# New step orders on all engines of a two-layer attention and expert kernel

## The reference, cut to what matters

```python
# layer 0, attention: 16 heads of width 128, a state per head
q, k, v = (silu(causal_conv(xn @ W.T, taps)) for W in (Wq, Wk, Wv))
beta = sigmoid(xn @ Wb.T);  q = l2norm(q) * hd**-0.5;  k = l2norm(k)
pred  = k_t @ state
state = state + k_t ^ (beta_t * (v_t - pred))        # for each token
o_t   = q_t @ state
out   = rmsnorm(o) * rms_w @ Wo.T
# layer 0, experts: 2 of 8 by a grouped router, and a shared one
# layer 1, attention: 2 heads, weights w0, w1, w2 learned on the way, chunks of 64
gate, hb = ki @ w0, ki @ w2;  hidden = silu(gate) * hb
w_m = w_m + newtonschulz5(gradient_m)                # 2 steps each, m = 0, 1, 2
w_m = w_m / (norm(w_m) + 1e-5) * norm(w_m at start)
oi  = silu(qi @ w0) * (qi @ w2) @ w1
out = rmsnorm(o) * onorm_w @ W_proj
# layer 1, experts: 2 of 6 for each whole sequence, gelu
```

## Time and profile before

| what | us |
|---|---|
| median of 3 runs | 1775.88 (1772.57 to 1785.23) |
| the profiled execution | 1781.47 |
| its span, first to last instruction | 1779.7 |
| PE busy | 1692.1 (95%) |
| DVE busy | 1470.7 (83%) |
| ACT busy | 1206.8 (68%) |
| POOL busy | 1104.7 (62%) |

### The profile page before, as it was taken

One profiled execution on the slowest core, in us unless ns is written; L12 is line 12 of the kernel. 1 busy time (PEld: TensorE's weight loads), 2 busy tenths in 40 slices (PEclk: granted clock), 3 DMA queues, 4 the chain that ended last, 5 costly groups with the idle time before them and its releaser, 6 DMA issues.

```text
span 1779.7 us, 41654 instructions
## 1 busy us (share of the span) xinstructions
PE 1692.1 (95%) x14070; PEld 1247.5 (70%) x14070; DVE 1470.7 (83%) x3684; ACT 1206.8 (68%) x2911; POOL 1104.7 (62%) x1148
## 2 busy tenths in 40 slices
PE   7999899999999999999999999999988788888888
PEld 5577567777777777777777777777767566666667
DVE  5322599999999999999999999999986788888863
ACT  2134477777777777777777777877754588778763
POOL 1600067777777777776666666666666478778841
PEclk9999999999999999999999999999986699999999
DMA  9433310111110110100001000101002000000033
GB/s 313 148 96 110 105 31 22 38 31 27 36 33 27 30 36 21 39 18 27 27 18 27 24 18 24 30 12 30 15 2 60 1 1 1 2 1 1 1 89 91
DMA packets 66098, 73.85 MB, mean 41 GB/s; under 512 B 10975, under 2 KB 54767, under 8 KB 65775
## 3 DMA queue, kind: packets, MB, share of 16 engines
q1 hardware_dynamic: 62919, 63.92, 12.2%
q0 software_dynamic: 3072, 8.65, 1.5%
HBM read 55.45 MB, written 17.10 MB: 41 GB/s over the span
## 4 chain that ended last, share of the span: by engine, by line
PE 84%; DVE 8%; ACT 5%; issue 1%; POOL 1%; SPq 0%; DMA 0%; POOLq 0%; DVEq 0%; ACTq 0%
PE banks L735 19%; PE banks L893 6%; PE banks L762 4%; PE banks L849 3%; PE banks L770 3%; PE banks L868 3%; PE banks L778 3%; PE banks L700 3%; PE banks L807 3%; PE banks L815 2%; PE banks L821 2%; PE banks L949 2%; PE banks L814 2%; PE banks L1025 2%; PE banks L719 2%; PE banks L960 2%
## 5 line engine op out<-in xcount | busy, mean ns | idle before, releaser
L735 PE MATMUL banks<-xnT,hw 128*128 128x512 f32 x768 | 414.1, 622 | 2.5 <-DVE cv L2034 2.5
L2090 DVE CAST_PREDICATED MM<-lmask,banks 128x512 bf16<-128x512 uint32 x384 | 272.5, 710 | 35.8 <-PE banks L815 31.5
L2034 DVE SCALAR_TENSOR_TENSOR cv<-banks,hc,cv 128x510 f32<-128x510 f32 (+2 forms) x384 | 284.8, 742 | 5.5 <-ACT cv L1439 0.8
L1503 ACT ACTIVATE T<-banks 128x256 bf16<-128x256 f32 x384 | 149.3, 389 | 147.4 <-PE banks L807 147.1
L2694 POOL TENSOR_TENSOR X<-X,yrow 128x512 f32<-128x512 f32 x128 | 163.3, 1276 | 66.3 <-ACT yrow L1535 66.3
L2658 POOL TENSOR_TENSOR kn<-nsum,half_pos 128x4 f32<-128x4 f32 x64 | 65.6, 1025 | 142.2 <-DVE nsum L2059 142.2
L815 PEld LDWEIGHTS banks<-MM,T 128*128 128x128 bf16 x1536 | 104.3, 98 | 65.4 <-issue 48.4
L814 PEld LDWEIGHTS banks<-T,MM 128*128 128x128 bf16 x1280 | 99.1, 97 | 65.3 <-ACT T L1503 63.1
L2034 DVE SCALAR_TENSOR_TENSOR cv<-banks,hcv,cv 128x510 f32<-128x510 f32 (+2 forms) x192 | 141.4, 736 | 1.4 <-ACT cv L1439 1.3
L893 PE MATMUL banks<-ho,OT 128*128 128x256 f32 x512 | 141.7, 400 | 0.0
L807 PEld LDWEIGHTS banks<-MM,Gb 128*128 128x128 bf16 x1536 | 84.2, 98 | 81.3 <-issue 43.7
(11 more groups left out here) (318 smaller groups left out, 4885.9 us busy)
## 6 DMA issues: line engine op xcount, KB each, us to landing
MM<-in_eye SPq DMA_DIRECT2D x64, 256.0 KB, 2.7
slot_rows<-zeros SPq DMA_DIRECT2D x1, 5304.0 KB, 20.1
xs<-slot_rows SPq DMA_DIRECT2D x13, 408.0 KB, 4.0
slot_out<-ye SPq DMA_DIRECT2D x13, 384.0 KB, 2.7
hw<-in_hw SPq DMA_DIRECT2D x16, 256.0 KB, 3.4
wT<-in_winit SPq DMA_DIRECT2D x8, 384.0 KB, 3.9
wgu<-in_wgu SPq DMA_DIRECT2D x1, 2816.0 KB
w1c<-in_ew SPq DMA_DIRECT2D x16, 176.0 KB
```

What stands on the lines that cost most here:

```text
L735: ins = pe.matmul(PROJ[t][:], hw[:, kk, t, :], xnT[:, kk, u.b * BLK:(u.b + 1) * BLK], start=(kk == 0), stop=(kk == KD - 1))
L1503: act.activation(strips(T1[:].rearrange("p i t -> p (i t)"), LEVELS[lv], 0, 1), grams_bank(u)[:, 0:TILES * 64].rearrange("p (k e) -> p k e ...
L2034: dve.scalar_tensor_tensor(o, y, taps_of(t)[:, TAPS - 1 - i:TAPS - i], o, ALU.mult, ALU.add).then_inc(dve_conv, 1)
L2090: dve.copy_predicated(dst, m, ps).then_inc(dve_mm, 1)
```

## The change

No instruction of the computation is added or taken away. The lists of steps are new: on PE, ACT, DVE and POOL in the first attention's period, in the last units and what lies between the stages, in the second attention's `pair_period`, and in the tail. Each list now also begins at another step of the cycle, so that a name such as `u3` can stand for the same unit as `u2` did. POOL's list goes up to two units further back (`mask`, `gram_rest` and the fetched rows come one period later), and its loop ends earlier, with `a59` and `a60` spelled out. `units` takes the number of units as an argument. Four waits are new: SP waits for all inversion steps before it loads the last pair's weights, `project_out` of the last two units waits for `act_ot`, `project_qk` of a first chunk waits for the turned rows itself, and POOL waits for its own addition of fetched rows.

```diff
-        def units(h, j):
-            return [unit(h, j, back) for back in range(5)]
+        def units(h, j, backs):
+            return [unit(h, j, back) for back in range(backs)]
...
             sp.wait_ge(*weights_loaded(2))
+            sp.wait_ge(pe_inv, 13 * UNITS)
             load_weights(3)
...
+                    pe.wait_ge(act_ot, u.n + 1)
                     if s == 1:
                         pe.wait_ge(act_bv, UNITS)
...
-                do(invert, u2, 5)
-                do(gram_keys, u1)
-                do(invert, u2, 6)
-                do(first_solve, u3, 1)
-                do(gram_second, u1)
+                u0, u1, u2, u3 = units(h, j, 4)
                 do(times_gram, u3, 1, 0)
                 do(invert, u2, 7)
                 do(project, unbegun(u0), QRY, 0)
                 do(invert, u2, 8)
+                do(correct, u3, 1, 0)
                 do(project, unbegun(u0), KEY, 0)
-                do(correct, u3, 1, 0)
                 do(invert, u2, 9)
                 do(project, unbegun(u0), QRY, 1)
...
+                do(invert, u1, 4)
                 do(correct, u2, 0, 1)
-                do(invert, u1, 4)
                 do(project_out, u3, 1)
                 do(carry, u2)
-
+                do(invert, u1, 5)
+                do(gram_keys, u0)
+                do(invert, u1, 6)
+                do(first_solve, u2, 1)
+                do(gram_second, u0)
             pe.wait_ge(a_const, 3 * 16)
             pe.wait_ge(*a_eye)
...
                     pe.wait_ge(t_wk2, u.n - NP + 1)
+                else:
+                    pe.wait_ge(ln_kept0, NBLK + u.p + 3)
...
+                do(newton, u3, 0, 0, NEXT)
+                do(newton, u4, 1, 1, GRAM)
+                do(grads, u2, 1)
+                do(newton, u4, 1, 1, SQUARE)
+                do(newton, u3, 0, 1, TURN)
+                do(project_v, u1)
+                do(newton, u4, 1, 1, NEXT)
+                do(newton, u3, 0, 1, GRAM)
+                do(turn_weight, u4, 0)
+                do(turn_output, u5)
+                do(total, u2)
                 do(newton, u3, 0, 1, SQUARE)
                 do(turn_qk, u1)
                 do(turn_weight, u4, 1)
-                do(project_rows, u5)
                 do(newton, u3, 0, 1, NEXT)
                 do(turn_v, u1)
+                do(project_rows, u5)
                 do(gate_queries, u4)
                 do(gates, u1)
                 do(newton, u3, 1, 0, TURN)
+                do(hidden_back, u1)
                 do(newton, u3, 1, 0, GRAM)
-                do(hidden_back, u1)
                 do(newton, u2, 0, 0, TURN)
                 do(newton, u3, 1, 0, SQUARE)
+                do(turn_weight, u4, 2)
                 do(turn_mixed, u4)
-                do(turn_weight, u4, 2)
+                do(newton, u2, 0, 0, GRAM)
                 do(newton, u3, 1, 0, NEXT)
-                do(newton, u2, 0, 0, GRAM)
+                do(project_qk, u0)
+                do(newton, u3, 1, 1, TURN)
+                do(newton, u2, 0, 0, SQUARE)
                 do(output, u4)
-                do(project_qk, u0)
-                do(newton, u2, 0, 0, SQUARE)
-                do(newton, u3, 1, 1, TURN)
                 do(grads, u1, 0)
-                do(newton, u3, 1, 1, GRAM)
-                do(newton, u2, 0, 0, NEXT)
-                do(grads, u1, 1)
-                do(newton, u3, 1, 1, SQUARE)
-                do(newton, u2, 0, 1, TURN)
-                do(project_v, u0)
-                do(turn_output, u4)
-                do(newton, u3, 1, 1, NEXT)
-                do(newton, u2, 0, 1, GRAM)
-                do(turn_weight, u3, 0)
-                do(total, u1)
             pe.wait_ge(t_const, 5 * 16)
...
+                do(keep_first, u3, 1)
                 do(silu, u1, VAL)
+                do(invert, u2, 4)
                 do(square_queries, u1)
                 do(invert, u2, 5)
                 do(cross_keys, u1)
+                do(gram_half, u1)
                 do(tap0, unbegun(u0), QRY)
-                do(gram_half, u1)
                 do(invert, u2, 6)
                 do(tap0, unbegun(u0), KEY)
+                do(first_queries, u1)
...
@@ -1693,95 +1706,94 @@
                 do(half_tanh, u1)
                 do(silu_gate, u1)
                 do(newton, u3, 1, 0, GRAM)
+                do(newton, u2, 0, 0, TURN)
+                do(keep_weight, u4, 2)
                 do(square_weights, u3, 0)
-                do(newton, u2, 0, 0, TURN)
+                do(newton, u2, 0, 0, GRAM)
                 do(keep_mixed, u4)
-                do(keep_weight, u4, 2)
-                do(newton, u2, 0, 0, GRAM)
+                do(newton, u3, 1, 1, TURN)
+                do(silu_qk, u0)
+                do(square_qk, u0)
                 do(square_outputs, u4)
-                do(silu_qk, u0)
-                do(newton, u3, 1, 1, TURN)
-                do(square_qk, u0)
...
                 do(key_inverse, u1)
                 do(invert, u2, 4)
                 do(key_scales, u1)
+                do(gram, u1, 0)
                 do(refine, u3, 1, 0)
-                do(gram, u1, 0)
                 do(gram, u1, 1)
...
-            residual(a62, 1, 1)
-            sum_qk(x0)
             refine(a62, 1, 1)
             rates_end(0)
+            norm_qk(x0, 0)
+            norm_qk(x0, 1)
+            residual(a63, 0, 0)
+            norm_qk(x0, 2)
+            refine(a63, 0, 0)
             norm_rows(1, 1)
-            residual(a63, 0, 0)
...
-                do(rhs_minus, u2, 0, 1)
-                do(inverse_rms, u3)
-                do(add_rows, u3, 0)
-                do(rhs_minus, u2, 1, 0)
-                do(first_rhs, u1)
-                do(root, u0)
-                do(mask, u1)
-                do(rhs_minus, u2, 1, 1)
-                do(add_rows, u3, 1)
-                do(gram_rest, u0)
-                if 0 <= i <= TOP0 * NT:
-                    do(rows_added, u3)
-                merge(i)
-                do(rhs_minus, u1, 0, 0)
-
+                u0, u1, u2, u3, u4, u5, u6 = units(h, j, 7)
+                do(add_squares, u5)
+                do(rhs_minus, u4, 0, 1)
+                do(inverse_rms, u5)
+                fetch_rows(i - 3)
+                do(rhs_minus, u4, 1, 0)
+                do(mask, u4)
+                add_fetched_rows(i - 4, u6, 1)
+                do(root, u2)
+                do(first_rhs, u3)
+                do(rhs_minus, u4, 1, 1)
+                fetched_rows_added(i - 4)
+                do(add_rows, u5, 0)
+                do(gram_rest, u3)
+                do(add_rows, u5, 1)
+                do(rhs_minus, u3, 0, 0)
             pool.wait_ge(a_const, 3 * 16)
             pool.wait_ge(m_added, 2 * NBLK)
...
             def pair_period(n):
                 u0, u1, u2, u3, u4, u5 = pair_units(n)
+                do(update, u4, 2)
+                do(root_grads, u2)
+                do(root_weights, u4, 1)
+                do(scale_weights, u4)
+                do(update, u3, 0)
+                do(update, u3, 1)
+                do(one_minus, u1)
+                do(rate_keys, u1)
+                do(root_weights, u3, 0)
                 do(rate_hidden, u1)
-                do(root_weights, u3, 0)
                 do(inverse_output, u4)
                 do(root_qk, u0)
                 do(scale_weights01, u3)
-                do(update, u3, 2)
-                do(root_grads, u1)
-                do(root_weights, u3, 1)
-                do(update, u2, 0)
-                do(update, u2, 1)
-                do(scale_weights, u3)
-                do(rate_keys, u0)
-                do(one_minus, u0)
             def weight_roots():
...
             rate_keys(x0)
             add_rows(a62, 0)
-            rhs_minus(a63, 1, 0)
-            rhs_minus(a63, 1, 1)
+            mask(a63)
             add_rows(a62, 1)
+            norm_root(2, 1)
             rate_powers(1)
             add_squares(a63)
-            norm_root(2, 1)
```

More of the change, by code:

```diff
@@ L2409, in gate_logits @@
                 dve.tensor_tensor(lg[:], lg[:], lmx[:].unsqueeze(2).to_broadcast([1, NB, E1]), ALU.subtract).then_inc(dve_once, 1)
+            tap(a63, VAL, 1)
+            invert(a62, 1)
+            square_sums(a60)
+            residual(a61, 0, 1)
+            refine(a61, 0, 1)
+            invert(a62, 2)
+            tap(a63, VAL, 2)
             second_rhs_half(a61)
```

582 lines of the change are left out of this document (310 added, 272 removed).

## The result

The changed kernel takes 1801.10 us in the median of 4 runs (1799.54 to 1807.90), the kernel before 1775.42 (1772.57 to 1785.23). The ratio is 1.0149, 95% interval 1.0105 to 1.0193. The forecast was 1767 us with a range to 1790, so it was wrong, and on the wrong side of no change. The profiled execution of the changed kernel took 1801.76 us, its span 1800.0 us, 20.3 us more than the span before.

What follows compares the result with a forecast made beforehand. It took the first attention as bound by PE, the second by a ring of waits, the stretch between by latency and a low clock. +5 - 17 + 3 = -9 us gave 1772.5 profiled, 1767 from the median; range 1747 to 1790.

Steps and rivals of the forecast that it cites:

- POOL in the first attention: First attention: mask, low Gram half and fetched rows come up to one period later; POOL has slack, so priced at nothing.
- Rival (B): Pair steps: DVE steps slowed beside POOL's updates give back 1.1 of 1.4 us each; about 1780 us, chance 0.17.
- PE's list: First attention: two moves put 128-column matmuls ahead of long float32 groups, 0.06 us less per unit, 4 us for 60.
- tap0 behind Gb: First attention, ACT: query tap 0.57 us later delays DVE; 0.15 us per unit reaches PE, 9 us, bounds 0 and 0.5.
- DVE's Gk ahead of the refinement: First attention, DVE: `gram` 0 ahead of a `refine` makes KX earlier but not the last Gk; no separate price.
- Sum for the first attention: PE's gain and the query tap's delay together: +0.09 us for each of 60 units, +5 us, bounds -4 and +26.
- Rival (C): First attention: DVE's 0.5 us delay behind the late query tap reaches PE whole; +26 us, about 1788 total, chance 0.13.
- The late weight load that costs nothing: First attention: a load waited 0.42 us for DVE at 712.59 while PE's long matmuls did not stop.
- Second attention: Pair steps: w1p ahead of squares and th, NEXT ahead of GRAM shorten the ring; 12 x 1.4 = 17 us less.
- The lower bound: Pair steps: gain of 0 if another order-bound ring of the old length takes over.
- Between the stages: Later rate power costs 4.9 us, `residual` ahead of row tiles gains 1.4; +3 us taken, bounds -3 and +7.
- Tail: End of the kernel: new order of nearly independent work, 0, within 2 us either way.

Runs made afterwards that it cites:

- e7: Kernel before with PE's two moves (correction, inversion step 4) and POOL's early key mask, in the first attention: units 17.87 us apart, ratio 1.0158.
- e12: Kernel before with POOL's early mask and only PE's correction moved ahead of the key projection: units 17.87 us apart, ratio 1.0162.
- e1: Changed kernel with POOL's key mask put back late in the first attention: units 17.62 us apart, ratio 1.0046 to the kernel before.
- e6: Kernel before with only PE's two moves (correction, inversion step 4) done in the first attention: units 17.40 us apart, ratio 0.9981.
- e18: e10 with PE's two moves (correction, inversion step 4) done in the first attention: 1750.90 us, ratio 0.9867 to the kernel before.
- e10: Kernel before up to pair step 2, changed kernel's pair steps and tail from pair step 3 on: 1754.45 us, ratio 0.9918.
- e2: Changed kernel with ACT's first query tap ahead of the half Gram matrix again: units 17.91 us apart, ratio 1.0138 to the kernel before.
- e17: Changed kernel with POOL's mask late and DVE's refinement ahead of the key-mask product again: units 17.50 us apart, ratio 0.9997 to the kernel before.
- e13: Changed kernel with POOL's mask, PE's two places and DVE's refinement put back: units 17.49 us apart, ratio 0.9989 to the kernel before.
- e5: Changed kernel with POOL's mask and PE's two places put back: units 17.63 us apart, ratio 1.0045 to the kernel before.
- e15: Kernel before with only DVE's first key-mask product moved ahead of the second chunk's refinement: units 17.59 us apart, ratio 1.0054.
- e11: Kernel before with only ACT's copy T of inversion step 3 moved behind both pieces of scaled rows: units 17.39 us apart, ratio 0.9992.
- e8: Changed kernel with two pieces between the stages put back (POOL's rate power; DVE's rates end and expert choice): ratio 1.0110 to the kernel before.
- e4: Kernel before with only POOL's key mask moved early in the first attention: units 17.50 us apart, ratio 1.0014.

## Why the prediction was wrong, point by point

**POOL in the first attention, "so I take nothing": the step that failed.** The prediction asked who reads the mask's result, and how busy POOL is. It did not ask which DVE step lies beside the mask at its new place. The named risk, that the mask would hold up `outputs`, was another one. The price is the wait at L821: 0.46 us a unit together with the moved correction (e7, e12), 0.29 in the changed kernel (e1). Rival (B) had the kind of effect, DVE beside POOL, but looked for it in the pair steps and at instructions of two SBUF inputs. In the trace a one-input step, 128x4, was stretched most. The trace of before already had such a case: `norm_qk` 0, which also adds a constant to 128x4 numbers, beside POOL's scaling of a weight. "SBUF — State Buffer" of the Trainium skill, section "SBUF: two separate sides", has a GpSimd instruction, and a VectorE instruction in a 2-port mode, take a shared pair of ports as an exclusive lock for the whole instruction; a VectorE instruction with two SBUF inputs does so against a GpSimd one that reads SBUF. By it `nsum` would wait for the mask's end; the trace agrees (1011.36 against 1011.32), but no run here shows in which mode that step runs.

**PE's list, -0.06 us a unit.** Alone it measured -0.01 to -0.02 (e6, and e18 against e10). No run shows the reason given, that the projection's weights can't be loaded behind so short a matmul. The prediction treated the moved correction as a matter of matmul shapes and did not look up how long its input had been ready. That was 0.76 us, a number that could have been read from the trace of before.

**tap0 behind Gb, +0.15 a unit.** Nothing in the changed kernel (e2), where PE waits at L821 anyway. DVE's first query tap waits 0.19 us for it and no more.

**DVE's Gk ahead of the refinement.** The prediction saw the move, took from it that KX is earlier, and gave no price to the refinement that now stands behind 0.6 us of Gk. It costs 0.12 to 0.17 us a unit (e17 against e1, e13 against e5, e15). Sum for the first attention: +5 predicted, with an upper bound of +26; +30 measured. The bound was too low because it was taken from one wait alone.

**Rival (C), 17.9 us apart and about 1788 or more.** Its sign came true, by a different cause; that (C) with (B)'s loss gave 1801, the measured time, is luck. The sign was therefore a bad one: it could not tell the mechanisms apart.

**The late weight load that costs nothing**, 0.42 us in the earlier trace rows, was read rightly: T's late load in e11 is a second case. What the reading missed is that Rb's lateness passes this cover. At L821 the load waits 0.45 us on the mean of 47 in e12's trace, and PE's matmul 0.34.

**Second attention, -17 us.** The size came true: 252.55 - 235.83 = 16.7 us, 1.39 for each of 12 periods where 1.4 was taken, at 19.65 us on the mean (19.7 predicted), PE at 94% (over 92% predicted). The mechanism is right in part, and no run takes its pieces apart. `square_weights` and w1p, which were on the chain of each period, are on it in none of the changed kernel's. But in 8 of the 12 periods, 19.2 us long, the chain there runs through another ring, over the squares of the gradients on ACT and their root on POOL (`root_grads`, gnb). Two rounds of it, start, us, what:

```profile
1504.19 2.45 POOL gnb L2786
...
1523.41 2.45 POOL gnb L2786
```

The lower bound had named such a ring, at the old length. And "DVE's part keeps its work: 0" missed `norm_qk` 0 (nq), 0.34 us shorter in the changed kernel. Before (with POOL's step beside one of them, 1463.03 to 1463.53) and changed:

```profile
L2232 DVE TENSOR_SCALAR nq<-nqr x16: 151/500/575, 1335.1 to 1674.5; 128x4 f32<-128x4 f32 x16
...
1461.47 2.04 POOL L2782 TENSOR_TENSOR wT<-wT,wsc 128x512 f32<-128x512 f32 x2
```

```profile
L2246 DVE TENSOR_SCALAR nq<-nqr x16: 150/161/171, 1370.3 to 1700.5; 128x4 f32<-128x4 f32 x16
```

So the fall of 1.39 on 1.4 is partly luck: the sum of the old ring is not what sets most of the new periods. Rival (B)'s `norm_qk` 2 takes 996 ns in the median, no more than before.

**Between the stages, +3 us, up to +7.** The sign of the loss was right, the size and most of the place were not. The rate power of pair 1 starts at 1392.17 with DVE waiting 5.28 us, as foretold; but counted from `keep_output` of unit 60 it starts at 67.6 us where it started at 54.8, 12.7 us later and not 4.9. Most of that is lost in the last three units. There the prediction took 1.4 us of gain from `residual` standing ahead of the row tiles. The single wait of 3.36 us for Rb did go, but the new order has PE wait 5.4 us for the inversion's merges where it waited 1.4, and the three units take 7.9 us more. In the two profiles the whole stretch is 8.9 us longer. Nine kernels with the old order here took 117.4 to 124.6 us (mean 120.1), ten with the new one 132.7 to 135.0 (133.8): 14 us. The profile of before had the longest of the nine, at the lowest granted clock (0.74, the others 0.78 to 0.81), which hid part of the loss. e8 explains 2.6 of the 14, the last three units hold some 8; which moves in them cost it is not settled.

**Tail, 0 within 2.** It gained 4.3 us against the profile of before. It takes 105.9 to 106.1 us in every kernel that has the new order there, 108.7 to 110.4 with the old one.

**The sum.** With the measured terms, 30 + 14 - 17 - 4 = +23 us, against 26 from the ratio (0.0149 x 1775). The gain in the pair steps was real; it was more than paid for in the first two stages.

## What to carry to other kernels

When a step is moved on one engine, write down for its new place which instructions of the other engines run beside it there (a step moved on POOL lengthened one on DVE from 0.17 to 0.83 us), and how much slack the next reader has; a move that eats slack and a move that needs it can each be nearly free alone (-0.01 and +0.09 us here, +0.46 together), and must be priced together. Read that slack from the trace as the distance from the end of the input to the start of its reader's load, for every step that is moved forward. An order by hand can be cut where two stages meet: taking the good stage of one version and the good stage of the other gave 0.8% here (e10), and 1.3% with PE's two places (e18), when the whole change lost 1.5%.

## What the runs showed of the hardware

A DVE `TENSOR_SCALAR` of 128x4 float32, 0.17 us alone, took up to 0.84 us beside a POOL step of two SBUF inputs of 128x512 (1.27 us), and ended with it, in the changed kernel (0.04 us behind); it was as long in e4. In the kernel before, another `TENSOR_SCALAR` of 128x4 took 0.50 us beside a POOL step of two SBUF inputs (1.04 us) and ended 0.02 us behind it, 0.16 us where no POOL step ran. A `SCALAR_TENSOR_TENSOR` that reads PSUM and one SBUF tile took 0.29 us beside the mask. A weight load that waits 0.2 us for its input between short matmuls cost nothing for each unit (e11), and one that waits 0.45 us on the mean, with PE's matmul waiting 0.34, cost 0.46 (e12).
